# Another order for every engine's pieces, and normalised rows on ScalarE, in a two-layer transformer kernel

## The reference

```python
x = x + L0_attn(layernorm(x))
x = x + L0_ffn(layernorm(x))
x = x + L1_attn(layernorm(x))
x = x + L1_ffn(layernorm(x))
```

```python
mem_out = (phi + phi ** 2) @ mem_w2          # phi = silu(q_mem @ mem_w1)
x = x + attn_out * sigmoid(mem_out)
y = rms_norm(x, norm2_w)
x = x + silu(y @ ffn_w1) * (y @ ffn_w3) @ ffn_w2     # 682 hidden
```

```python
act = silu(xf @ w1_gate) * (xf @ w1_up)
out = sum_e combine[t, e] * act[e] @ w2[e]  + shared
```

## Time and profile before

| | before |
|---|---|
| runs, device us | 773.07, 778.89, 772.74 |
| median | 773.07 |
| profiled execution, its own time | 772.71 |
| its span in the trace | 770.9 |
| TensorE's mean granted clock | 0.931 |
| TensorE busy | 688.9 us (89%) |
| VectorE busy | 422.6 us (55%) |
| ScalarE busy | 313.1 us (41%) |
| GpSimd busy | 259.0 us (34%) |

### The profile page before, as it was taken

How to read it: one execution, slowest core, us unless ns; L and a number is a source line. 1 busy time by engine, 2 the same in 40 slices (tenths; PEclk the granted TensorE clock), 3 DMA queues, 4 the chain that set the end, 5 groups by cost and what they waited for, 6 DMA issues and landing times.

```text
span 770.9 us, 13166 instructions
## 1 busy us (share of the span) xinstructions
PE 688.9 (89%) x5188; PEld 560.3 (73%) x5188; DVE 422.6 (55%) x896; ACT 313.1 (41%) x748; POOL 259.0 (34%) x334
## 2 busy tenths in 40 slices
PE   4799999998898799958599988998699999999997
PEld 3565867765787587947476866776588888888886
DVE  5755687632348676464565555554553545454445
ACT  3340734534333242414476766566243232222322
POOL 4313232521425722221735343333314333433400
PEclk9977899987998699979799999899899999999999
DMA  6322100100112200000100000000043343333111
GB/s 207 94 69 72 50 3 2 29 2 1 50 42 61 62 1 22 0 21 22 41 2 21 1 2 2 1 1 1 2 118 111 99 132 105 96 116 124 60 37 55
DMA packets 18637, 37.32 MB, mean 48 GB/s; under 512 B 2544, under 2 KB 4720, under 8 KB 18576
## 3 DMA queue, kind: packets, MB, share of 16 engines
q1 hardware_dynamic: 18576, 36.48, 15.4%
HBM read 35.19 MB, written 1.11 MB: 47 GB/s over the span
## 4 chain that ended last, share of the span: by engine, by line
PE 71%; DVE 14%; ACT 7%; issue 5%; POOL 3%; DMA 1%; DVEq 0%; SPq 0%; POOLq 0%; ACTq 0%
PE ps L612 46%; PE ps L755 3%; PE ps L937 3%; PE ps L731 3%; PE ps L925 3%; PE ps L915 2%; PE ps L634 2%; PE ps L690 2%; ACT AO L1214 2%; PE ps L638 2%; PE ps L620 1%; DVE NB L1281 1%; PE ps L629 1%; ACT HHh L1131 1%; PE ps L705 1%
## 5 line engine op out<-in xcount | busy, mean ns | idle before, releaser
L1807 POOL TENSOR_SCALAR PB<-PB,sml 128x256 f32<-128x256 f32 x128 | 59.2, 482 | 94.2 <-DVE sml L1623 94.2
L1131 ACT CAST VVh<-U 128x512 fp32r<-128x512 f32 x50 | 31.1, 621 | 118.3 <-DVE U L1469 104.8
L612 PE MATMUL ps<-ATh,wh 128*128 128x512 f32 x176 | 71.9, 409 | 3.0 <-issue 1.4
L1461 DVE TENSOR_TENSOR U<-U,ps 128x512 f32<-128x512 f32 x50 | 34.4, 688 | 67.2 <-PE ps L612 67.2
L612 PE MATMUL ps<-ATl,wh 128*128 128x512 f32 x176 | 70.7, 402 | 0.0
L612 PE MATMUL ps<-ATh,wl 128*128 128x512 f32 x176 | 70.4, 400 | 0.0
L1776 POOL TENSOR_SCALAR wh<-wr 128x768 fp32r<-128x768 f32 (+3 forms) x31 | 24.1, 779 | 129.3 <-PE ps L612 126.3
L1202 ACT ACTIVATE PB<-ps,sml 128x256 f32<-128x256 f32 x128 | 59.5, 492 | 7.8 <-DVE sml L1617 7.7
L1778 POOL TENSOR_TENSOR wl<-wr,wh 128x768 fp32r<-128x768 f32 (+3 forms) x31 | 56.6, 1825 | 2.6
L1473 DVE TENSOR_TENSOR VVl<-U,VVh 128x512 fp32r<-128x512 f32 x50 | 34.6, 693 | 36.9 <-ACT VVh L1131 36.9
L1214 ACT COPY AO<-ps 128x512 f32<-128x512 f32 x64 | 35.0, 589 | 48.0 <-PE ps L925 47.8
(11 more groups left out here) (290 smaller groups left out, 2043.4 us busy)
## 6 DMA issues: line engine op xcount, KB each, us to landing
wr<-in_w SPq DMA_DIRECT2D x32, 384.0 KB, 3.1
wr<-in_w SPq DMA_DIRECT2D x16, 321.0 KB, 2.9
CB<-weights_of_experts SPq DMA_DIRECT2D x16, 256.0 KB, 3.9
wr<-in_w SPq DMA_DIRECT2D x11, 256.0 KB, 2.6
CB<-weights_of_experts SPq DMA_DIRECT2D x8, 224.0 KB, 3.5
CB<-weights_of_experts SPq DMA_DIRECT2D x8, 192.0 KB, 3.3
CB<-weights_of_experts SPq DMA_DIRECT2D x8, 160.0 KB, 3.4
XO<-in_x SPq DMA_DIRECT2D x2, 512.0 KB, 4.7
```

The lines of the kernel that those rows point to most:

```text
L612: t = x.matmul(o, a, b, start=first and i == 0 and c == 0, stop=last and i == n - 1 and c == 2, skip_group_check=skip)
L1131: x.copy((VV if run == "moe" else HH)[c][0][:, :], b[:, :]).then_inc(*mark("hi", "h", run, j, half))
L1461: x.tensor_tensor(b[:, :], a[:, :], bank("u", run, j, half)[:, :], ALU.mult).then_inc(*vacates("u", run, j, half))
L1807: t = x.tensor_scalar(p[:, c, :], p[:, c, :], m[:, 16 + c:17 + c], 1.0, ALU.mult, ALU.mult)
```

## The change

New lists PROLOGUE, PERIOD and LAST put the pieces of every engine in another order, from the prologue to the first units of L1_attn. No piece is added or dropped in them. What ScalarE, VectorE, GpSimd and TensorE do from L1_attn's unit 5 on keeps its order, except for endnorm.

The rows of memscale, ffnnorm, latnorm and endnorm are made by ScalarE instead of VectorE. A scale is r2 or rs as before; a bias, sh = -mean x rs, is added: VectorE writes ng = -mean (in `variance`), and GpSimd multiplies it by rs (in `rsqrt`). memscale has a scale alone. The rows of norm1 stay on VectorE. For half 1, endnorm's VectorE and GpSimd parts keep their place and its ScalarE part stands behind the first step of moe ("step moe 0 0"); for half 0 the piece stays where it is in the loop, for all engines.

What else moves, engine by engine, as far as it matters later: GpSimd does consts ahead of norm1. TensorE does project 0 ahead of fuse 1, turnqk 0 ahead of fuse 6, score 0 1 ahead of project 2. In the periods the projections of the next batch but one stand a place later, and parted 0 1 and 1 1 on ScalarE behind the last exponential of the batch after. In the last batch ScalarE's step mem 0 0 stands behind expo 3 3 and oproj 3 instead of ahead of expo 3 2, and TensorE's behind oproj 3 and expo 3 2; parted 3 1 stands ahead of step mem 2. memnorm on VectorE stands ahead of step mem 5 1, and memturn behind down mem 6 1. In the start of L1_attn GpSimd's order is: split moe0, expert 1, l1norm 0, latstd 1, split moe1, l1norm 1 (before: expert 1, split moe0, split moe1, l1norm 0, latstd 1, l1norm 1), VectorE does l1exp 1, l1exp 2 and l1norm 0 ahead of ffndown 1 and latstd 1, and latq 0 1 stands ahead of up 1.

The diff, with the lists cut to the parts that are spoken of:

```diff
 PROLOGUE = [
-    "fuse@v 2", "norm1@a 0", "norm1@a 1", "norm1@g 0", "consts", "turn1@p 0", "norm1@v 0", "turn1@a 0", "fuse@v 0",
-    "fuse@p 0", "fuse@p 1", "turn1@v 0", "fuse@a 1", "tables", "clear", "project@p 0", "fuse@p 2", "fuse@v 1",
-    "project@v 0", "rope@v 0", "fuse@p 3", "fuse@a 0", "project@a 0", "fuse@v 3", "project@p 1", "fuse@a 3",
-    "project@a 1", "rope@g 0", "project@v 1", "headnorm@a 0", "fuse@v 4", "project@g 0", "fuse@a 4", "fuse@a 8",
-    "fuse@p 4", "rope@v 1", "fuse@a 5", "fuse@p 5", "finish@g 0", "finish@a 1", "fuse@p 6", "project@g 1",
-    "headnorm@v 0", "finish@v 1", "rope@g 1", "finish@v 0", "finish@g 1", "norm1@g 1", "fuse@a 7", "fuse@v 5",
-    "fuse@p 7", "finish@a 0", "norm1@v 1", "fuse@v 8", "turnqk@p 0", "fuse@v 7", "turnqk@a 0", "turnqk@v 0", "fuse@a 9",
...
+    "fuse@v 2", "norm1@a 0", "consts", "turn1@p 0", "norm1@v 0", "turn1@a 0", "tables", "norm1@g 0", "fuse@p 0",
+    "fuse@v 0", "fuse@a 1", "project@a 0", "turn1@v 0", "fuse@v 1", "project@p 0", "fuse@v 3", "clear", "fuse@p 1",
+    "rope@g 0", "fuse@p 2", "fuse@a 0", "norm1@a 1", "rope@v 0", "fuse@a 3", "fuse@p 3", "project@p 1", "fuse@v 4",
+    "project@a 1", "project@v 0", "headnorm@a 0", "fuse@a 4", "project@g 0", "rope@v 1", "fuse@p 4", "finish@g 0",
+    "fuse@a 8", "fuse@a 5", "finish@a 1", "finish@a 0", "fuse@p 5", "project@v 1", "headnorm@v 0", "turnqk@p 0",
+    "project@g 1", "rope@g 1", "finish@v 1", "finish@v 0", "finish@g 1", "fuse@v 5", "fuse@p 6", "turnqk@a 0",
+    "norm1@g 1", "fuse@p 7", "fuse@a 7", "fuse@v 8", "fuse@p 8", "norm1@v 1", "fuse@v 7", "fuse@p 9", "turnqk@v 0",
...
 ]
 PERIOD = [
-    "expo@a 0 0", "rope@g 2 0", "project@g 2 0", "turnqk@a 1 0", "turnqk@v 1 0", "expo@p 0 0", "rope@v 2 0",
-    "expo@a 0 1", "turnqk@p 1 0", "project@v 2 0", "project@a 2 0", "expo@p 0 1", "rope@g 2 1", "expo@p 0 2",
-    "score@v 1 0", "project@p 2 0", "parted@g -1 1", "score@p 1 0", "turnqk@p 1 1", "turnqk@v 1 1", "expo@a 0 2",
-    "turnqk@a 1 1", "expo@p 0 3", "expo@a 0 3", "project@p 2 1", "score@p 1 1", "project@v 2 1", "score@p 1 2",
-    "weigh@p 0 0", "expo@p 0 4", "expo@p 0 5", "score@v 1 1", "rope@v 2 1", "parted@a -1 1", "score@v 1 2",
...
+    "expo@a 0 0", "rope@g 2 0", "turnqk@v 1 0", "expo@p 0 0", "turnqk@a 1 0", "turnqk@p 1 0", "expo@a 0 1", "expo@p 0 1",
+    "rope@g 2 1", "project@v 2 0", "project@p 2 0", "expo@p 0 2", "score@v 1 0", "project@a 2 0", "score@p 1 0",
+    "turnqk@v 1 1", "expo@a 0 2", "turnqk@a 1 1", "turnqk@p 1 1", "expo@p 0 3", "project@g 2 0", "rope@v 2 0",
+    "project@p 2 1", "score@p 1 1", "project@g 2 1", "parted@g -1 1", "project@v 2 1", "score@v 1 1", "score@p 1 2",
+    "weighed@g 0 0", "rope@v 2 1", "weigh@p 0 0", "expo@a 0 3", "project@a 2 1", "expo@a 0 4", "score@v 1 2",
+    "expo@p 0 4", "expo@p 0 5", "headnorm@v 2 0", "score@v 1 3", "headnorm@a 2 0", "score@p 1 3", "score@p 1 4",
...
 LAST = [
-    "expo@a 3 0", "l0last", "expo@p 3 0", "parted@a 2 1", "oproj@p 0", "oproj@a 0", "expo@p 3 1", "expo@a 3 1",
-    "oproj@p 1", "oproj@a 1", "mlpbegin", "step@p mem 0 0", "step@a mem 0 0", "step@v mem 0 0", "expo@p 3 2",
-    "expo@a 3 2", "oproj@a 2", "expo@a 3 3", "oproj@p 2", "oproj@a 3", "oproj@p 3", "parted@g 2 1", "expo@p 3 3",
...
-    "memadd@a 3", "memadd@v 3", "step@a mem 5 1", "step@v mem 5 1", "down mem 2 1", "split ffn2", "memnorm@v 0",
-    "memnorm@g 0", "step@p mem 6 1", "step@a mem 6 1", "step@v mem 6 1", "down mem 3 1", "split ffn3", "memscale 0",
-    "step@p mem 7 1", "step@a mem 7 1", "down mem 4 1", "down mem 5 1", "split ffn4", "memturn@p 0", "memturn@a 0",
-    "step@v mem 7 1", "memturn@v 0", "memturn@g 0", "down mem 6 1", "split ffn5", "down mem 7 1", "split up",
...
-    "split gate", "l1score 0", "latq@p 0 1", "latq@a 0 1", "latq@v 0 1", "expert@a 1", "l1exp@v 0", "expert@v 1",
-    "expert@g 1", "split moe0", "expert@p 1", "l1exp@a 0", "l1score 1", "l1rings", "latq@p 0 2", "latq@a 0 2",
-    "latq@v 0 2", "ffndown@v 1", "l1exp@v 1", "split moe1", "l1exp@a 1", "l1exp@v 2", "l1norm@v 0", "ffndown@p 1",
-    "l1norm@g 0", "l1score 2", "latstd@v 1", "latstd@g 1", "latnorm 1", "l1norm@g 1", "l1exp@a 2", "l1turn@p 0",
-    "l1turn@a 0", "l1norm@v 1", "l1score 3", "latq@p 0 3", "latq@a 0 3", "l1turn@p 1", "l1turn@a 1", "l1exp@a 3",
-    "l1exp@v 3", "latq@p 1 0", "latq@v 0 3", "l1norm@v 2", "l1norm@g 2", "latq@a 1 0", "latq@v 1 0", "l1score 4",
...
+    "parted@a 2 1", "oproj@p 0", "oproj@a 0", "expo@p 3 0", "expo@a 3 0", "expo@a 3 1", "oproj@a 1", "expo@a 3 2",
+    "l0last", "oproj@p 1", "expo@p 3 1", "oproj@a 2", "oproj@p 2", "parted@g 2 1", "expo@a 3 3", "oproj@p 3",
+    "oproj@a 3", "mlpbegin", "expo@p 3 2", "step@p mem 0 0", "step@a mem 0 0", "step@v mem 0 0", "expo@p 3 3",
...
+    "step@a mem 4 1", "memadd@a 2", "step@v mem 4 1", "memadd@v 2", "split ffn1", "memadd@a 3", "step@p mem 4 1",
+    "step@a mem 5 1", "memadd@v 3", "memnorm@v 0", "split ffn2", "memscale 0", "memnorm@g 0", "split ffn3",
+    "step@p mem 5 1", "step@v mem 5 1", "down mem 2 1", "step@p mem 6 1", "step@a mem 6 1", "step@v mem 6 1",
+    "down mem 3 1", "split ffn4", "step@p mem 7 1", "step@v mem 7 1", "step@a mem 7 1", "down mem 4 1", "memturn@a 0",
+    "down mem 5 1", "memturn@v 0", "memturn@g 0", "down mem 6 1", "memturn@p 0", "down mem 7 1", "split ffn5",
+    "memadd@a 4", "memadd@v 4", "step@p ffn 0 0", "step@v ffn 0 0", "step@a ffn 0 0", "step@p ffn 1 0", "step@a ffn 1 0",
...
+    "latrest@a 0", "latrest@v 0", "up@a 1", "split gate", "latq@p 0 1", "l1score 0", "latq@a 0 1", "split moe0",
+    "up@v 1", "latq@v 0 1", "expert@a 1", "up@p 1", "expert@p 1", "l1exp@v 0", "expert@v 1", "expert@g 1", "l1exp@v 1",
+    "l1score 1", "l1rings", "latq@p 0 2", "latq@a 0 2", "l1exp@a 0", "latq@v 0 2", "l1exp@v 2", "l1norm@v 0",
+    "l1exp@a 1", "ffndown@v 1", "l1norm@g 0", "ffndown@p 1", "latstd@g 1", "l1score 2", "latstd@v 1", "l1exp@a 2",
+    "l1turn@p 0", "l1exp@v 3", "l1turn@a 0", "l1score 3", "latq@p 0 3", "split moe1", "l1norm@v 1", "l1norm@g 1",
+    "latnorm 1", "l1norm@g 2", "latq@a 0 3", "l1turn@p 1", "l1turn@a 1", "latq@p 1 0", "latq@v 0 3", "l1norm@v 2",
+    "l1exp@a 3", "l1norm@g 3", "l1hi 0", "l1score 4", "l1weigh 0", "latq@a 1 0", "latq@v 1 0", "l1turn@p 2",
...
@@ -362,14 +362,15 @@
         item("l1" + kind, n - d)
     item("l1add", 3)
     item("moebegin")
-    item("endnorm", 1)
+    item("endnorm@v", 1)
+    item("endnorm@g", 1)
     split(9)
 
     def moe_after(half):
         return [[("store", 4 * half + c)] for c in range(4)]
 
     rest = mlp("moe", [f"moe{j}" for j in range(25)], 3, 1,
-               [[], [], [("endturn", 1, 0), ("endturn", 1, 1)], [("gate", 1), lambda: freed("gate")]], moe_after,
+               [[("endnorm@a", 1)], [], [("endturn", 1, 0), ("endturn", 1, 1)], [("gate", 1), lambda: freed("gate")]], moe_after,
                {(1, 0): [("spread", 0)], (0, 1): [("route", 1)], (1, 1): [("spread", 1)]})
     for p in rest:
         item(*p[0])
@@ -418,6 +419,8 @@
     mv = sb("mv", [128, NT, 2])
     ve = sb("ve", [128, NT])
     rs = sb("rs", [128, NT])
+    ng = sb("ng", [128, NT])
+    sh = sb("sh", [128, NT])
     r2 = sb("r2", [128, NT])
     v2 = sb("v2", [128, NT])
     masks = AO[:, :, :].rearrange("p t d -> p (t d)")[:, 0:896]
@@ -491,7 +494,7 @@
 
     order, us = plan()
     n_units = len(us)
-    gated = [tuple(o[2:]) for o in order if o[0] == "step" and o[1] == "moe" and o[2] >= 3]
+    gated = [tuple(o[2:]) for o in order if o[0] in ("step", "step@v") and o[1] == "moe" and o[2] >= 3]
     cb = small("cb")
     SC = float(1.0 / np.sqrt(128.0))
     xv = x.rearrange("(t p) d -> p t d", p=128)
@@ -1219,6 +1222,26 @@
             e.wait_ge(*have("lw", i))
             x.copy(UT[0][:, i % 4, :], bank("lw", i)[:, 0:256]).then_inc(*mark("hi", "u", i))
 
+        def normalize(half, of, kind):
+            e.wait_ge(*at(of, half))
+            for t in range(half * 4, half * 4 + 4):
+                x.activation(NB[:, t, :], XO[:, t, :], ACT.Identity, scale=rs[:, t:t + 1], bias=sh[:, t:t + 1]).then_inc(
+                    *mark(kind, t))
+
+        def memscale(half):
+            e.wait_ge(*at("r2m", half))
+            for t in range(half * 4, half * 4 + 4):
+                x.activation(NB[:, t, :], X1[:, t, :], ACT.Copy, scale=r2[:, t:t + 1]).then_inc(*mark("rdm", t))
+
+        def ffnnorm(half):
+            normalize(half, "sh2", "rn")
+
+        def latnorm(half):
+            normalize(half, "sh3", "rl")
+
+        def endnorm(half):
+            normalize(half, "sh4", "re")
+
         def endturn(half, k):
             turn(("te", half, k), AT, half, k)
 
...
@@ -1273,6 +1297,8 @@
         def variance(half, kind):
             hs = slice(half * 4, half * 4 + 4)
             e.wait_ge(*now("dv"))
+            if kind != "ve":
+                x.tensor_scalar(ng[:, hs], mv[:, hs, 0], -1.0, None, ALU.mult)
             x.tensor_scalar(ve[:, hs], mv[:, hs, 1], 1e-5, None, ALU.add).then_inc(*mark(kind, half))
 
```

(9 more changed lines are left out.)

20 lines of the change are left out of this document (9 added, 11 removed), and 73 rows, old and new, of tables (LAST, PERIOD, PROLOGUE).

## The result

The changed kernel is 0.9% faster: its ratio to the kernel before is 0.9914, with a 95% interval of 0.9891 to 0.9937, from 20 runs of each (medians 762.93 and 771.63 us). That is 6.6 us, with 4.9 to 8.4 by the interval, where 18.5 were forecast (the ratio of the two medians alone would be 0.9887, or 8.7 us); the profiled execution took 762.40, with a span of 760.6. The time lies 8.4 us above the forecast of 754.5, and the baseline hides a little more of the miss: three runs gave a median of 773.07, and every later set of 11 or more gave 768.9 to 771.6.

The account below looks back on a forecast made before the run. TensorE bounds: a busy final 214 us at full clock, before it stops behind other engines' chains and half clock. Terms summing to 18.5 us off 772.71 gave 754.2, plus 0.36 to the runs' median: 754.5 us, range 743 to 768.

Parts of the forecast that it names:

- prologue 0.5: Prologue: masks built while GpSimd waits for x, TensorE pieces reordered; net gain 0.5 us (-4 to +7).
- last attention 5.0: Last attention: step mem 0 0 moved behind unit 3 shortens the 2.89 us stop and recovers clock; gain 5.0 us (0 to 6.5).
- after it 1.0: After the last attention: parted 3 1 ahead of step mem 2 lets mem3's split come earlier; gain 1.0 us (-1 to 2).
- memscale 0 3.5: memscale 0: rows on ScalarE take about 1.8 instead of 5.5 us, beside VectorE's hidden values; gain 3.5 us (1 to 6).
- ffnnorm 0 0.8: ffnnorm 0: rows on ScalarE win 1.0 us, sh costs 0.25; gain 0.8 us.
- latnorm 0 -0.6: latnorm 0: VectorE was free there, so ScalarE's slower rows and sh lose 0.6 us.
- start of l1 2.5: Start of L1_attn: reordered splits and exponentials bring the first turn up to 6 us earlier, the second less; gain 2.5 (0 to 8).
- endnorm 0 -1.6: endnorm 0, in the l1 loop: QHh waits behind sh and ScalarE's rows, delaying TensorE; loss 1.6 us (-2.6 to +2.3).
- endnorm 1 7.4: endnorm 1: product U no longer waits behind VectorE's blocked rows; 5.8 us of stop and 1.6 of clock, gain 7.4 (5 to 8).
- 4 of the 5.1 come back: Last attention: of 5.1 us of work lost to clock 0.81 over 27 us, 4 would be regained.
- rival "slower": Rival: the new order lowers TensorE's clock over the first 192 us, from 0.87 to 0.80 or less; about 785 us, chance 0.05.
- less: Rival: the orders give nothing at the start of l1 or the last attention; about 762 us (760 to 765), chance 0.22.

Follow-up runs that it names:

- e13: Changed kernel with one wait added: GpSimd's clears begin only when VectorE's norm1 rows, half 0, are written; ratio 0.9878 to the kernel before.
- e2: Kernel before with one piece moved: GpSimd makes the masks (consts) ahead of norm1; ratio 1.0035 to the kernel before.
- e4: Changed kernel with the three old lists, so the rows alone are on ScalarE in the old orders; ratio 1.0029 to the kernel before.
- e3: Changed kernel's new lists with all rows of memscale, ffnnorm, latnorm and endnorm back on VectorE; ratio 1.0026 to the kernel before.
- e17: Changed kernel with the rows of memscale, ffnnorm, latnorm and endnorm 0 back on VectorE, only endnorm 1's on ScalarE; ratio 0.9899 to the kernel before.
- e7: Changed kernel with TensorE's step mem 6 0 moved behind down mem 0 1, as the kernel before has it; ratio 0.9901 to the kernel before.
- e8: Changed kernel with GpSimd's split of moe1 behind l1norm 2 and VectorE's l1norm 1 ahead of l1exp 3; ratio 0.9888 to the kernel before.
- e5: Kernel before with only endnorm 1's rows on ScalarE, behind step moe 0, in the old orders; ratio 0.9899 to the kernel before.
- e1: Changed kernel with GpSimd's two buffer clears moved right behind consts, ahead of norm1; ratio 0.9887 to the kernel before.

## Why the prediction was wrong

The direction was right; the size was not even half. It predicted a mechanism for each site, and the sum failed at four terms: the prologue, what comes after the last attention, the start of l1, and the last attention's share of clock. Forecast and measured, by stretch (means where several executions share the orders), and what TensorE's idle time gave of it; the rest is clock and a few matmuls that changed stretch:

```
stretch, its terms in the sum              forecast   measured   idle
A  prologue 0.5, periods 0                      0.5       -4.8   -5.3
B  last attention 5.0                           5.0        3.9    2.5
C  after it 1.0, memscale 0 3.5                 4.5        0.2   -0.6
D  ffnnorm 0 0.8                                0.8        2.7    1.6
E  latnorm 0 -0.6                              -0.6       -1.0   -0.5
F  start of l1 2.5                              2.5       -0.1    2.3
G  endnorm 0 -1.6                              -1.6       -2.1   -1.6
H  endnorm 1 7.4                                7.4        7.1    5.7
I  none                                         0         -0.6   -0.6
```

The measured column adds up to 5.3, close to the 6.6 by the runs.

- **The prologue, 0.5.** The step "GpSimd builds the masks while it waits for x" stopped one piece too soon. What stood behind the masks moved forward too, and that was two clears of 1.9 us, put beside the rows of norm1. I had argued from this very collision at three other sites and did not look for new ones. 3.2 us, shown by e13 and e2. The rest is mostly the 2.3 us of idle time up to 60 us: I had counted 1.2 against the new order there and balanced it with gains that did not come. The Trainium skill, SBUF — State Buffer, says that GpSimd and VectorE arbitrate for one shared pair of ports, held for a full instruction; the trace agrees, with 1.98 us for an instruction of 0.41 beside a clear of 1.90.
- **memscale 0 and the work after the last attention, 3.5 and 1.0.** The rows did give, and about what I forecast: TensorE's idle time in C is 14.0 us on average with the old orders and VectorE's rows and 10.8 with ScalarE's (e4), 17.7 with the new orders and VectorE's rows (e3, e17) and 14.2 to 14.8 with both new. So the rows gave some 3 us in either order, and the new orders took some 3.7 with either rows; in length, C is 77.2 in e4, 80.0 on average before, and 81.9 and 83.0 in e3 and e17. I costed the moved memnorm and transposes as gains. But down mem 5 1, which stands in front of the transposes in both orders, waits for the hidden value of step mem 5 1, and that is now behind memnorm on VectorE (in e3 behind the rows as well). The stop ahead of that down, before, in changed and in e3:

```profile
247.71 0.58 PE L612 MATMUL ps<-xh,HHh 128*128 128x256 f32 x1 [3.73 <-DVE HHl L1473]
```

```profile
248.55 0.58 PE L615 MATMUL ps<-xh,HHh 128*128 128x256 f32 x1 [6.63 <-DVE HHl L1499]
```

```profile
255.69 0.58 PE L613 MATMUL ps<-xh,HHh 128*128 128x256 f32 x1 [11.06 <-DVE HHl L1474]
```

  With the waits for NB behind it, 2.57 the first, the stops there added up to 9.4 before; in changed 6.63 and 1.66 make 8.3. Most of the wait had moved, not gone. And mem6, whose weights take the place that oproj 7 reads last, had lost its cover: stops of 2.54 and 0.93 are new there; e7 shows that giving it back only moves that wait again.
- **The start of l1, 2.5.** The first turn did come early, and I had named the risk ("latstd 1 now stands ahead of moe1's split"). And TensorE's idle time in F did fall by 2.3, so the waits were right in size. What the term left out was the clock, which I had named for the second turn alone: TensorE needed 2.1 us more for the same matmuls, as it now worked through time at half clock of which it had spent a part idle before. From 373.4 to 376.8 us, behind the second stop, changed runs at half clock; in e8, where l1norm 1 no longer waits behind moe1's split, such a stretch is gone, and F is 3.1 shorter. What brings such a stretch on is not shown: F of e7 is 1.4 shorter than that of changed in the same order.
- **The last attention, 5.0,** was right in kind: the stop of 2.89 is gone, and unit 5 waits 1.2 in ten of the 14 executions, as I had it. In size it is 3.9, because "4 of the 5.1 come back" leaned on the clock of one execution; the clock gave 1.4, the waits 2.5 where I had 1.0.
- **endnorm 1, 7.4**, was right in place, mechanism and size (7.1), **endnorm 0, -1.6**, was right in its stop (5.08 for 3.51), and **latnorm 0, -0.6**, a little too kind: ScalarE's group with a bias takes 2.07, above the upper bound of 2.0 that I had worked out from a scale alone. A scale alone takes 1.71, close to my 1.75.
- **ffnnorm 0, 0.8**, came out at 2.7, and not by its rows: D is 32.4 with them on VectorE too. It is the new order that puts ScalarE's and VectorE's pieces of step ffn 1 1 ahead. Of the 2.7, idle time is 1.6; 1.1 are matmuls that the new order has in other stretches, so no gain.
- **The clock.** The profiled execution of before had a poor one in the prologue. From 40 to 100 us, before, and then e5, whose orders are the same there:

```profile
40.00:100.00 60.00, 57.18 (x422) 40.33 (x424) 35.74 (x84) 23.10 (x58) 14.59 (x23) 0.79 0.21 61
```

```profile
40.00:100.00 60.00, 56.55 (x580) 40.69 (x579) 42.19 (x97) 25.48 (x63) 16.39 (x26) 0.94 0.21 58
```

  I read 0.87 over 192 us as a property of the kernel and put upsides and a rival on it. Over these 192 us the profiles with the old PROLOGUE read 0.85 to 0.90 and those with the new one 0.85 to 0.92, so neither its size nor its place tells much of the kernel. The rival "slower" also took idle time for work: of the 192 us TensorE was busy 166.75, and these partly at half clock, so less than 167 us of work at full clock stood in them.

Of the rivals, "less" comes nearest: the orders as a whole gave nothing (e3, e17), and 762 was its number. That the number fits is luck, though. It had 0 for the last attention, which gave 3.9, and 0 for the start of l1 by a new wait of GpSimd's, where the waits did shrink; the losses in A and C, which made up for that, are not in it. I gave it 0.22 and the forecast 0.48; its warning that sites "trade one wait for another" held at memscale 0 and at mem6. (A slip beside it: 773.07 less 18.5 is 754.57, not 754.5.)

## What to carry to other kernels

When a piece moves forward on a queue, follow what stands behind it to the next wait, and ask what that will now run beside; on GpSimd above all, whose long memsets and splits held VectorE's rows and low parts here for their whole length. Moving one group off a blocked engine was worth 7 us, the other seven and three rewritten lists together nothing more, so try the site with the long stop alone first. Compare idle times as well as lengths: what a wait cost shows in one trace, while the clock needs several. Read a clock that differs from stretch to stretch in one execution as luck until a second execution shows the same.

## What the hardware showed that I had not expected

- A GpSimd memset, which reads nothing, holds VectorE's normalised rows and conversion just as a split does: 1.57 us instead of 0.42 for a 128x512 instruction (e1), 1.98 instead of 0.41 for a 128x256 one. Not every instruction is held: at 5.57, beside the same clear, a reduction of VectorE's took its usual 0.16 (e1).
- On ScalarE the rows with scale and bias read from SBUF took 589 ns, those with a scale alone 498, for 128x256. They differ in function too (Identity and Copy), so that the 90 ns are the bias is likely and not shown.
- The clock falls to half for some 3 us with TensorE busy throughout. Changed kernel, 500 to 503 us, and 496 to 499 for comparison:

```profile
500.00:503.00 3.00, 3.00 (x15) 2.34 (x12) 1.39 (x5) 0.07 (x1) 1.45 (x4) 0.50 0.00 0
496.00:499.00 3.00, 3.00 (x33) 2.87 (x30) 0.42 (x1) 2.35 (x10) 0.42 (x1) 1.00 0.00 0
```

  Such a stretch of 3.4 us (499.7 to 503.1) costs about 1.7 us, and B, C and I differ between executions of the same orders in steps of about that size (I: 202.7 and 204.3). So a fall needs no stop, though I had written at endnorm 1 that with no stop the clock has no cause to fall.
